# A pipelined attention and mixture-of-experts block: the gates of a tile are loaded one expert pair per slot, and each engine's loop carries a branch hint

## The reference

```
expert_out = einsum('bnd,edc->bnec', t, expert_w) + expert_b
out = y + sum over the best two experts of gate * expert_out
```

## Time and profile before

| | us |
|---|---|
| three runs, median (lowest to highest) | 3749.16 (3746.48 to 3774.52) |
| the profiled execution, its own time | 3730.37 |
| the span of its profile | 3728.5 |
| DVE busy | 3190.4 (86%) |
| PE busy | 3199.5 (86%) |
| POOL busy | 2942.7 (79%) |
| ACT busy | 2233.5 (60%) |

### The profile page before, as it was taken

How to read it: one execution, slowest core, us unless ns; L and a number is a source line. 1 busy time by engine, 2 the same in 40 slices (tenths; PEclk the granted TensorE clock), 3 DMA queues, 4 the chain that set the end, 5 groups by cost and what they waited for, 6 DMA issues and landing times.

```text
span 3728.5 us, 203806 instructions
## 1 busy us (share of the span) xinstructions
PE 3199.5 (86%) x82757; PEld 1956.7 (52%) x82757; DVE 3190.4 (86%) x6174; ACT 2233.5 (60%) x4514; POOL 2942.7 (79%) x5385
## 2 busy tenths in 40 slices
PE   3889989988898888898889888888889888989884
PEld 1655555555555555555555555555555555555541
DVE  2789989998999989998889988888889988889983
ACT  2676666666666656665566656665556666666640
POOL 3988878888888878887788878877788878788860
PEclk8999999999999999999899999999899989999996
DMA  1245455555455545555545555545455545455545
GB/s 27 60 97 126 117 123 121 129 120 122 118 127 121 124 109 129 115 127 115 120 110 127 122 117 121 125 111 122 113 120 125 124 115 123 114 116 126 125 104 126
DMA packets 415302, 432.05 MB, mean 116 GB/s; under 512 B 129984, under 2 KB 395888, under 8 KB 414320
## 3 DMA queue, kind: packets, MB, share of 16 engines
q1 hardware_dynamic: 248432, 304.94, 36.0%
q0 software_dynamic: 165888, 113.57, 12.9%
HBM read 245.79 MB, written 58.98 MB: 82 GB/s over the span
## 4 chain that ended last, share of the span: by engine, by line
PE 36%; SPq 23%; issue 15%; DVE 14%; DMA 5%; ACT 3%; POOL 2%; DVEq 0%; ACTq 0%; POOLq 0%
SPq L397 13%; PE bank L628 8%; PE bank L564 7%; DVE lepe L899 4%; SPq L429 4%; PE bank L549 3%; PE bank L641 3%; PE bank L584 2%; SPq L455 2%; DVE gx L887 2%; PE bank L633 2%; DMA gate_rows<-gateT 2%; DVE row_max L907 2%; DMA z<-fin 2%; PE bank L653 2%
## 5 line engine op out<-in xcount | busy, mean ns | idle before, releaser
L504 POOL DMA_DIRECT2D vx<-vt x3072 | 1561.7, 517 | 414.1 <-PE bank L633 403.3
L628 PEld LDWEIGHTS bank<-probT,vx 128*32 128x32 f32 x36864 | 824.6, 189 | 464.5 <-issue 452.8
L628 PE MATMUL bank<-probT,vx 128*32 128x16 f32 x36864 | 886.3, 234 | 159.2 <-issue 144.0
L493 POOL DMA_DIRECT2D kx<-k_sb x1536 | 741.0, 489 | 229.5 <-issue 102.8
L564 PEld LDWEIGHTS bank<-kx,qx 32*32 32x32 f32 x36864 | 584.9, 110 | 443.6 <-issue 441.3
L564 PE MATMUL bank<-kx,qx 32*32 32x64 f32 x36864 | 689.3, 223 | 133.3 <-issue 111.1
L899 DVE SCALAR_TENSOR_TENSOR lepe<-vpad,lepe_sb,lepe 128x384 f32<-128x384 f32 x960 | 673.5, 702 | 0.8 <-issue 0.8
L718 ACT ACTIVATE prob<-prob 128x512 f32<-128x512 f32 x576 | 367.4, 638 | 288.1 <-DVE prob L912 285.0
L887 DVE TENSOR_TENSOR gx<-gate_wide,yn_pair 128x768 f32<-128x768 f32 x384 | 397.4, 1036 | 112.9 <-PE bank L549 62.1
L523 POOL TENSOR_TENSOR lepe_p<-lepe_p,tap_sb 128x384 f32<-128x384 f32 x384 | 434.9, 1133 | 32.7 <-issue 11.3
L912 DVE TENSOR_TENSOR prob<-bank,row_max 128x512 f32<-128x512 f32 x576 | 398.4, 692 | 16.7
(11 more groups left out here) (87 smaller groups left out, 4517.8 us busy)
## 6 DMA issues: line engine op xcount, KB each, us to landing
gate_wide<-gate_rows SPq DMA_DIRECT2D x384, 384.0 KB
vx<-vt POOLq DMA_DIRECT2D x3072, 12.0 KB
kx<-k_sb POOLq DMA_DIRECT2D x1536, 24.0 KB
yn_pair<-yn POOLq DMA_DIRECT2D x384, 96.0 KB
z<-fin SPq DMA_DIRECT2D x1344, 24.0 KB
xs<-in_x SPq DMA_DIRECT2D x96, 192.0 KB
xt<-in_x SPq DMA_DIRECT2D x192, 96.0 KB
z0t<-z SPq DMA_DIRECT2D x192, 96.0 KB
```

Of the source, the lines that this page charges most:

```text
L493: pool.dma_start(kx[to + m:to + C:4, r % 2, m, :], k_sb[at + m:at + C:4, r % 2, :])\
L504: pool.dma_start(vx[to:to + TOK, r % 2, g * 8 + x:g * 8 + 8:2, odd, :], vt[at:at + TOK, r % 2, x::2, :, :].rearrange("p h n k -> p h (n k)"))\
L628: last = MM(bank_o[32 * c:32 * c + 32, at * TOK:(at + 1) * TOK], vx[:, kr % 2, :, at % 2, at // 2 * 4 + c], probT[:, kr % 2, at, c * TOK:( ...
```

## The change: what it does

1. **Gates per pair.** `spread_gates` moves from lag 41 to 40 and is done in four slots, 6k+40 to 6k+43, one expert pair in each. A pair is two DMAs of 64 partitions x 2 x 384, so a tile has eight DMAs of half the size instead of four; the bytes are the same. Pair p waits only until pair p's product of the tile before is made. `GATE_DMAS` becomes 8, also in what DVE waits for ahead of pair 0. DVE's code is otherwise the same.
2. **Place in SP's list.** `store_gates` and `spread_gates` now stand behind `load_pair` and ahead of `store_z` in a slot; before they stood behind `load_tile`.
3. **Hint.** The loop over passes is opened with a hint for its closing branch, one instruction at the top of each engine's loop body.

```diff
-    take_logits=34, ..., store_gates=39, spread_gates=41,
+    take_logits=34, ..., store_gates=39, spread_gates=40,
...
-    with eng.Fori(0, turns) as turn:
+    with eng.bass.Fori(0, turns, engines=[eng.engine], hint_back_edge=True) as turn:
...
-        ..., GATE_DMAS = 5, 11, 7, 8, 16, 4
+        ..., GATE_DMAS = 5, 11, 7, 8, 16, 8
...
+                if ti := s.tile("store_gates"):
+                    k, r = ti
+                    wait_alone(sp, gateT_saved, k + 1)
+                    if s.later(r, 2):
+                        wait_alone(sp, gate_spread[r % 2], k // 2 * (GATE_DMAS * 16))
+                    sp.dma_start(gate_rows[r % 2], gateT[:, r % 2, :]).then_inc(gate_stored[r % 2], 16)
+                if (ti := s.in_tile("spread_gates")) and ti[2] < PAIRS:
+                    k, r, p = ti
+                    if p == 0:
+                        wait_alone(sp, gate_stored[r % 2], (k // 2 + 1) * 16)
+                    if s.later(r, 1):
+                        wait_alone(sp, gx_made, (k - 1) * PAIRS + p + 1)
+                    by_expert = gate_rows[r % 2].rearrange("(f p e) n -> e p f n", f=2, e=2)
+                    for odd in range(2):
+                        sp.dma_start(gate_wide[odd * C:(odd + 1) * C, p, :, :],
+                                     by_expert[odd, p].unsqueeze(0).broadcast_to([C, 2, SPX]))\
+                            .then_inc(gate_spread[r % 2], 16)
                 if st := s.strip("store_z"):
...
-                if ti := s.tile("store_gates"):
...
-                if ti := s.tile("spread_gates"):
-                    k, r = ti
-                    wait_alone(sp, gate_stored[r % 2], (k // 2 + 1) * 16)
-                    if s.later(r, 1):
-                        wait_alone(sp, gx_made, k * PAIRS)
-                    by_expert = gate_rows[r % 2].rearrange("(f p e) n -> e f p n", f=2, e=2)
-                    for odd in range(2):
-                        for half in range(2):
-                            sp.dma_start(gate_wide[odd * C:(odd + 1) * C, :, half, :],
-                                         by_expert[odd, half].unsqueeze(0).broadcast_to([C, PAIRS, SPX]))\
-                                .then_inc(gate_spread[r % 2], 16)
```

More of the change, by code:

```diff
@@ L70 @@
     store_z=15, load_tile=24, y_first=28, y_second=29, tile_sum=30, tile_variance=31, router=32, logits=33,
-    take_logits=34, gates=36, gap_exp=37, turn_gates=38, pair_yn=38, store_gates=39, spread_gates=41,
+    take_logits=34, gates=36, gap_exp=37, turn_gates=38, pair_yn=38, store_gates=39, spread_gates=40,
     expert_bias=43, products=44, experts=45, tile_out=47)
@@ L315, in metaformer_block @@
         N_WEIGHT_DMAS = 1 + 3 + 16 + 2 + 12 + 4 + 2
-        X_DMAS, Z_DMAS, TILE_DMAS, K_DMAS, V_DMAS, GATE_DMAS = 5, 11, 7, 8, 16, 4
+        X_DMAS, Z_DMAS, TILE_DMAS, K_DMAS, V_DMAS, GATE_DMAS = 5, 11, 7, 8, 16, 8
         block = ctx.enter_context(nc.Block())
```

## The result

The changed kernel took 4827.38 us (median of 4, 4795.55 to 4834.75) against 3747.82 us (median of 4) for the kernel before: a ratio of 1.286, 95% interval 1.278 to 1.294. The direction was forecast, the size was not: 4440 us, in a range from 4270 to 4700. In all that follows the times are medians of all timed executions, while the ratios leave out the slow ones, those more than 1.5% above the fastest of the same kernel: four of twelve in e1, one of six in e11, none elsewhere.

What follows compares the result with a forecast made beforehand. DVE, PE and SP were taken as balanced at 37.4 us a tile. 3730.4 + 730 (new chain, 88 tiles) + 15 - 24 - 14 - 8 = 4429 us, median put at 4440; range for 8 in 10: 4270 to 4700.

Steps and rivals of the forecast that it cites:

- The chain: Slot 0's `fin`, SP's z stores and x loads, pair 3, pair 0's product: 23.7 us a tile, 10.9 before.
- The landing of pair 3: From pair 3's first issue on SP to its data's arrival: 4.6 us, bounds 3.5 and 7.
- the stall: DVE standing still ahead of pair 0's product, waiting for gates: some 8 to 12 us in each tile.
- The sum: Profiled time plus all terms, 4429 us, from a period of 45.7 us a tile against 37.4.
- the SP legs: From slot 0's `fin` over SP's issues to pair 3's issue: 0.8 + 18.0 + 0.25 us.
- Y: Part of a tile from pair 0's product to the next slot 0's `fin`: 22 us, ends 20.9 and 24.
- the correction for the slots around the loop: Z stores take 7.54 us, not 9, in slots written out around the loop: 16 tiles shorter by 1.5 us, -24.
- the 8 us taken for the hint: Branch hint removes issue waits at the loop's jumps back: between 0 and -14 us, taken as -8.
- Rival 2: PE, idle in each stall, resumes at 1.2 GHz: +264 us, some 4700 us; chance 0.12.
- Rival 3: SP's own work closes the ring, 24 us instead of 21.6: period 47.7, +175 us, 4615 us; chance 0.08.
- Rival 1: Pair 3 lands in time for pair 0's product, so not slower: median some 3705 us; chance 0.06.
- the price of 50 ns per issue: Skill page's dispatch cost for one DMA: SP's 25 issues would take 1.3 us; the forecast used 0.82 per z issue.

Runs made afterwards that it cites:

- e1: The kernel before with the branch hint alone: 3734 us, ratio 0.993.
- e11: Changed kernel, gates loaded in two halves (slot 5, and slot 0 ahead of the z stores) with 6 KB rows: 3552 us, 0.947 of the kernel before.
- e5: Changed kernel, pair 3 issued behind pair 2 in slot 0, ahead of the z stores: 3668 us, 0.979 of the kernel before.
- e2: Changed kernel, the two x loads of 62 partitions each split into 32 and 30: 4559 us, 1.218 of the kernel before.
- e10: Changed kernel without the branch hint: 4833 us, 1.289 of the kernel before.
- e9: The kernel before, gate loads carrying pair 0 alone (a quarter of the bytes), all four products reading its gates: 3490 us, ratio 0.932.
- e8: The kernel before with the branch hint and the store of the gates issued ahead of slot 3's z stores: 3799 us, ratio 1.016.

## Why the prediction was wrong, point by point

- **The chain** from `fin` over SP's list to pair 3 and pair 0's product was right: e5 removes it and the loss with it. Its legs on SP came out at 19.4 us in the tile shown, 19.2 in the mean, against 19.05.
- **The landing of pair 3** is the step that failed. It was put at 4.6 us with an upper end of 7; it is 8.7 us in the tile shown and 9.15 in the median. The estimate itself was good for a load on free engines (e2: 4.4). The error was in the bound: I took what stands ahead of pair 3 as bytes spread over 16 engines, from a load of 64 partitions, and didn't look at the shapes of the five loads ahead of it in the list, 62 partitions each for two of them. While their packets pass, two at a time, pair 3's last packets come behind them, and DVE waits for the last of those. So the term was too small by 4.5 us a tile, some 400 us over 88 tiles, and the stall was 14.7 us in the mean instead of 8 to 12.
- **The sum.** The period is 49.3 us, from pair 0's product of tile 0 (270.47) to tile 88's (4607.36), over 88. I had 45.7: the landing adds 4.5, the SP legs 0.2, and Y came out at 21.1 us in the mean instead of 22. 88 x 3.6 = 317 us, of the 366 between my 4429 and the profiled 4795.55; another 24 are the correction for the slots around the loop, which the measured period holds already. The rest is about the 8 us taken for the hint, the period before (37.34 us, rounded to 37.4), and some 13 us ahead of tile 0's product and in the last tiles.
- **Rival 2, the clock**, had the clock right and its price wrong. In the tile shown the granted clock is 1.00, that is 2.4 GHz, until some 6 us into the stall, then 0.50, that is 1.2 GHz, and full again some 5 us behind pair 0's product; its mean over the span is 0.827, against 0.923 before. PE is busy 90 us longer, 1 us a tile. But the way from pair 0's product to slot 3's `fin`, at 0.50 for the most part, takes 4.72 us, exactly as in the earlier trace rows, and Y as a whole, 21.1 us, is shorter than the 22.3 us mean of before. So the lower clock did not lengthen the period here.
- **Rival 3**: SP waited for `fin` 1245.1 us, most of it in slot 3. In slot 0, which the rival named, it stood only some 1 us ahead of the z stores in the median: it did not close the ring by itself, but little was missing. **Rival 1** and the price of 50 ns per issue fall with SP's rows: 9.37 / 11 = 0.85 us.
- **The rest**: SP's waits for gate_rows disappeared (7.6 us left), and the last three tiles turned in 14.4 us each against 14.8 forecast. The hint was sized at -8; neither e1 nor e10 shows an effect clear of the noise. DVE and PE are busy 64% and 69% instead of 72%. The four added gate issues were priced at 0.85 us each, and cost SP 2.5 us a tile together: an issue of half the bytes takes SP as long as one of the whole (0.63 against 0.62 us in the median).

## What to carry to other kernels

When a wait counts several transfers, ask which of them is issued last and what stands ahead of it in the issuer's list; two loads issued 23 places later cost 1160 us here (e5 against the changed kernel). A load can be held up by a transfer ahead of it that few DMA engines carry, so look at the partition counts of the transfers ahead of it, and read the DMA share: here it stayed at 0.13 to 0.17, near 2/16, while DVE waited, and splitting the transfers of 62 partitions took 4.7 us off the landing. And a large load that nobody is seen to wait for can still cost, by what it holds back (e9).

## What the runs showed of the hardware that I had not expected

- Two x loads of 62 partitions keep two of sixteen DMA engines busy for four us (share 0.13 to 0.17), and splitting them into 32 and 30 halves the landing of what comes behind, 9.15 to 4.4 us.
- Loading a quarter of the gates' bytes made the kernel before 6.8% faster, though DVE waits for them only 1.3% of the span.
- In the kernel before, 222 us of TensorE's waits end some 1.5 us behind the landing of a 16 KB packet of instructions, nearly all close behind the gate loads. With a quarter of the bytes it is 50 us (e9).
- Freeing SP of a wait (e8) made the kernel 1.6% slower.
- After a stall in which the granted clock fell to 0.50, PE was busy 90 us more over the span, but Y was 21.1 us against 22.3 before.
